# A two-layer decoder step in one Trainium2 kernel: in the second cross attention, VectorE takes the low part of each query projection one tile later

## What is computed

```
q = (queries @ Wq).reshape(b, s, KV_HEADS, GROUP, HEAD_DIM)   # 8, 4, 16
k = (keys @ Wk).reshape(b, s, KV_HEADS, HEAD_DIM)
v = (values @ Wv).reshape(b, s, KV_HEADS, HEAD_DIM)
scores = einsum('bqhgd,bkhd->bhgqk', q, k) * scale
attn = softmax(scores, axis=-1)
out = einsum('bhgqk,bkhd->bqhgd', attn, v).reshape(b, s, 512)
x = x + out @ Wo
```

## Time and profile before

| | |
|---|---|
| median of three runs | 2592.67 us (2592.54 to 2593.83) |
| the profiled execution, its own time | 2595.24 us |
| span of the profile | 2593.5 us |
| mean granted TensorE clock | 0.975 of full speed |
| busy: PE, PEld, DVE, ACT, POOL | 2462.0, 2090.9, 1304.4, 935.9, 732.1 us |
| the second cross attention's four pairs in the trace | about 2330 to 2547 us |

### The profile page before, as it was taken

How to read it: one execution, slowest core, us unless ns; L and a number is a source line. 1 busy time by engine, 2 the same in 40 slices (tenths; PEclk the granted TensorE clock), 3 DMA queues, 4 the chain that set the end, 5 groups by cost and what they waited for, 6 DMA issues and landing times.

```text
span 2593.5 us, 39558 instructions
## 1 busy us (share of the span) xinstructions
PE 2462.0 (95%) x13371; PEld 2090.9 (81%) x13371; DVE 1304.4 (50%) x2997; ACT 935.9 (36%) x2495; POOL 732.1 (28%) x434
## 2 busy tenths in 40 slices
PE   5999899999999999977799999999999999998897
PEld 3788788889888888966688888888888888875665
DVE  6444444444444444564544444444444444567675
ACT  2111344444444444430233333333333333336672
POOL 4245432222322223221211111121111211126660
PEclk9999899999999999988899999999999999997998
DMA  3110221111211121101111111111111111100000
GB/s 111 57 45 28 90 81 49 65 49 56 74 49 65 49 73 57 53 21 43 41 43 42 42 42 42 42 42 42 42 42 42 42 42 42 59 1 1 1 1 33
DMA packets 36976, 119.49 MB, mean 46 GB/s; under 512 B 4920, under 2 KB 7352, under 8 KB 36928
## 3 DMA queue, kind: packets, MB, share of 16 engines
q1 hardware_dynamic: 36928, 118.88, 13.0%
HBM read 116.76 MB, written 2.10 MB: 46 GB/s over the span
## 4 chain that ended last, share of the span: by engine, by line
PE 86%; DVE 7%; issue 3%; POOL 2%; ACT 2%; SPq 0%; DMA 0%; DVEq 0%; POOLq 0%; ACTq 0%
PE pj L521 18%; PE pj L522 18%; PE pj L523 18%; PE ou L521 6%; PE ou L523 6%; PE ou L522 6%; PE sc L655 2%; PE sc L757 2%; PE pv L766 2%; PE pv L671 2%; DVE probs L1257 1%; PE tp L662 1%; PE tp L872 1%; POOL w_lo L393 1%; PE sc L521 1%
## 5 line engine op out<-in xcount | busy, mean ns | idle before, releaser
L385 POOL TENSOR_TENSOR w_lo<-raw,w_hi 128x1024 fp32r<-128x1024 f32 x144 | 344.5, 2392 | 1451.1 <-ACT w_hi L968 1451.1
L521 PE MATMUL pj<-xt_hi,w_hi 128*128 128x512 f32 (+2 forms) x1296 | 519.4, 401 | 7.6 <-POOL w_lo L393 2.0
L522 PE MATMUL pj<-xt_lo,w_hi 128*128 128x512 f32 (+2 forms) x1296 | 502.5, 388 | 0.0
L523 PE MATMUL pj<-xt_hi,w_lo 128*128 128x512 f32 (+2 forms) x1296 | 501.6, 387 | 0.0
L521 PEld LDWEIGHTS pj<-xt_hi,w_hi 128*128 128x128 f32 x1296 | 246.8, 190 | 54.3 <-issue 6.2
L521 PE MATMUL ou<-w_hi,act_hi 128*128 128x512 f32 x684 | 275.4, 403 | 13.1 <-DVE act_lo L1495 4.8
L523 PEld LDWEIGHTS pj<-xt_hi,w_lo 128*128 128x128 f32 x1296 | 245.8, 190 | 49.8
L522 PEld LDWEIGHTS pj<-xt_lo,w_hi 128*128 128x128 f32 x1296 | 246.9, 191 | 41.8
L1216 DVE TENSOR_TENSOR x<-x,ou 128x512 f32<-128x512 f32 (+1 forms) x200 | 136.3, 685 | 285.0 <-PE ou L523 285.0
L523 PE MATMUL ou<-w_hi,act_lo 128*128 128x512 f32 x684 | 268.5, 393 | 0.0
L522 PE MATMUL ou<-w_lo,act_hi 128*128 128x512 f32 x684 | 268.0, 392 | 0.0
(11 more groups left out here) (247 smaller groups left out, 4902.0 us busy)
## 6 DMA issues: line engine op xcount, KB each, us to landing
raw<-in_l1a_w SPq DMA_DIRECT2D x80, 512.0 KB, 4.8
raw<-in_l0x_w SPq DMA_DIRECT2D x64, 512.0 KB, 3.4
side<-in_side SPq DMA_DIRECT2D x32, 512.0 KB, 3.7
raw<-in_ffn_w SPq DMA_DIRECT2D x15, 512.0 KB, 3.2
raw<-in_l1x_w SPq DMA_DIRECT2D x7, 512.0 KB, 3.4
raw<-in_l0f_w SPq DMA_DIRECT2D x6, 512.0 KB, 3.9
raw<-in_taylor_w SPq DMA_DIRECT2D x5, 512.0 KB, 6.6
x<-in_x SPq DMA_DIRECT2D x2, 1024.0 KB, 6.6
```

Of the source, the lines that this page charges most:

```text
L385: pool.tensor_tensor(WL[:, s, :], RAW[:, s, :], f32(WH[:, s, :]), ALU.subtract).then_inc(w_ready[s], 1)
L521: pe.matmul(out, wh, xh, start=first, stop=False)
L522: pe.matmul(out, wh, xl, start=False, stop=False)
L523: return pe.matmul(out, wl, xh, start=False, stop=last)
```

## The change

VectorE's call of `queries` moves by one step in each of its four places in a boundary between pairs: c0 from step 11 to step 12, c1 from 13 to 14, c2 from 15 to step 0 of the next pair, and c3 from step 1' to step 2'. It stands, as before, behind `turned_lo` of its step and ahead of `heads`, `dequantise` and `add`. The index of c2's call is 2 in the next pair in place of 6 in the former: the same projection, bank and columns. No instruction is added or removed; ScalarE, TensorE, GpSimd and SyncE keep their orders. Three boundaries with four calls each make 12 instructions that move.

```diff
@@ -1656,10 +1656,10 @@
                     row_recip(m)
                     if not (first and m < 2):
                         turned_lo(m - 2)
-                    if m == 1 and not first:
-                        queries(3)
-                    if m in (11, 13, 15) and not last:
-                        queries(KC + (m - 11) // 2)
+                    if m in (0, 2) and not first:
+                        queries(2 + m // 2)
+                    if m in (12, 14) and not last:
+                        queries(KC + (m - 12) // 2)
                     if m == 3 and not first:
                         heads(-1)
                     if m == 11:
```

## The result

The changed kernel takes 2581.97 us (median of five runs, 2580.19 to 2584.34) against 2592.67 us (five runs, 2589.14 to 2594.57): 10.7 us less by the medians. The ratio is 0.9955, with a 95% interval of 0.9944 to 0.9967, which is 8.6 to 14.5 us. Forecast were 11.1 us and 2581.6. Its profiled execution took 2582.41 us, with a span of 2580.6, 12.9 us less than before's profiled one.

What follows compares the result with a forecast made beforehand. TensorE bounds the kernel; its boundary waits and lags (10.2 + 1.1 + 0.8) make 12.1 us. Less 3 x 0.34 kept by GpSimd's cycle, the gain is 11.1: 2592.67 - 11.1 = 2581.6 us, range 2577.6 to 2588.

Steps and rivals of the forecast that it cites:

- R: Rival in the single-stall experiments: VectorE's idle time counts, each stall by its share of a boundary's 9.8 us; no chance given.
- (1): VectorE's 12 moved low parts, one step later, wait for nothing: 0 us each, bounds 0 and 0.2.
- (2): First stall, step 12: TensorE's transposes follow their scores after 0.89 us, so the 0.97 us are gone entirely.
- (3): Second stall, 4.33 us under the output projection: its cost shows two steps later, in step 15; 1.9 us gained so far.
- (4): Stalls three and four: GpSimd's 2.33 us cycle leaves 0.34 us a boundary; scores of step 5 start 4.0 us earlier.
- (5): Later readers of the moved low parts on TensorE: cover of 7, 4.5, 4.6 and 3.4 us for c0 to c3.
- (6): Left as they are: waits of 0.63 and 0.37 us inside pairs 1 and 2, and all outside the stretch.
- The rule weighed: VectorE and GpSimd share a port pair: `neg_max` waits for GpSimd's product, 0.99 instead of 0.17 us; without it, 2580.6 us.
- Rival A: Steps 12 to 4': GpSimd's cycle takes over, `neg_max` held in all nine; gain 5.5, 2587.2 us; chance 14%.
- C: TensorE's transposes wait for GpSimd's product or the exponentials instead of `turned_lo`; gain near 0, 2592 us; chance 12%.
- B: Step 15's wait stays, made by `add(0)`; gain 8.5, 2584.2 us; counted within the forecast's case, 69% together.
- D: VectorE steps 12, 14, 0, 2: low part delays `row_max`, `neg_max` meets GpSimd product; 9.1 us slower, 2601.8 us; chance 5%.

Runs made afterwards that it cites:

- ScalarE earlier: Against the kernel before: VectorE's order kept, ScalarE makes each high part one step earlier (10, 12, 14, 0); 2582.89 us, ratio 0.996.
- doubled low part: Against the changed kernel: each of the 12 moved low parts computed twice, the first time into memory that nothing reads; 2581.78 us, ratio 0.9956.
- two steps later: Against the changed kernel: low parts one step later still (steps 13, 15, 1, 3); 2580.38 us, ratio 0.9953.
- no `neg_max`: Against the changed kernel: `neg_max` and its semaphore removed, query projections scaled by -1/4, row minimum as bias of the exponentials; 2581.17 us, ratio 0.9954.
- `add` later: Against the changed kernel: in pairs 1 and 2 the addition of the former pair's last output moves from step 6 to step 10; 2580.43 us, ratio 0.9949.
- both: Against the changed kernel: `neg_max` removed and, in pairs 1 and 2, add(-1) moved from step 6 to step 10; 2582.33 us, ratio 0.9957.

## Why the prediction was right, step by step

- **The bound.** That only TensorE's waits can be won held: 10.97 us were won at the boundaries of the 12.1 counted there, and R, which counts VectorE's 27.0 us, fell in both directions (c1 0.9 a boundary for 4.33 us of stall, c3 1.3 for 1.73). The 12.1 itself was 0.3 too high: the 10.97 won and the 0.80 kept (below) make 11.8, as the lags outside the boundary that was read were smaller than the 0.25 estimated.
- **(1) The stall goes, for 0 us.** The 12 waits have no row after; `turned_lo` and the low part run back to back at 2424.33 and 2424.93, and ScalarE's high part had ended at 2424.56, 0.37 us before the low part starts. That nothing but the high part's coming first matters is shown by the run with ScalarE earlier.
- **(2) and (3).** Step 12: 0.97 forecast, 0.97 measured at the second boundary. Up to step 15: 1.9 us forecast, 1.86 measured (0.97 in step 12, 0.86 in step 15 and 0.03 between).
- **(4) The rest.** 4.0 forecast, 4.01 measured at the second boundary. What was kept back, 0.34 us, was in fact one wait of 0.23 (0.29 by the starts); the lags of 0.11 and 0.15 in steps 3 and 4 did not come. At the first and third boundary the measured 3.47 and 3.49 are what their brackets and lags gave, less the one wait for keys that stayed (0.29 and 0.22 by the starts). So 0.80 us was kept in all, not 1.02. The sum of 11.1 against 10.97 is right by its terms, but that it comes within 0.1 us is luck: 0.3 too much counted and 0.2 too much kept back. That the medians, which scatter by a few us, differ by just 10.7 is luck too.
- **(5) The readers.** Cover of 7, 4.5, 4.6 and 3.4 us was forecast, and the trace of the changed kernel has 7.1, 4.6, 4.6 and 3.5 at the second boundary. Two steps of delay against the kernel before are free, and three cost 5.0 to 5.2 us a boundary beyond the change where the clock stays up. Right.
- **(6).** The 0.63 and 0.37 us inside the pairs stayed to the hundredth.
- **The rule weighed.** `neg_max` is held by GpSimd's products less than I thought: of the nine in steps 12 to 4' of the second boundary five took 0.17 us and four 0.33 to 0.45. The sign that I named, `neg_max` near 1 us more often, went the other way: eight lasted 0.99 to 1.04 us in the stretch of the earlier trace rows, and two in the changed kernel's 123 us. Rival A's cycle ran in four of the nine steps, 0' and 2' to 4', where GpSimd's products stand 2.32 or 2.33 us behind the last (rows of steps 2' to 4' below, timeline of POOL, changed kernel), and TensorE lost 0.29 us to it. By the Trainium skill's rule that I named ("SBUF — State Buffer", Who interferes with whom) the second to issue blocks until the first is done, and the trace agrees: the lengthened `neg_max` of step 3' ends at 2446.31, 0.03 us behind GpSimd's product for the keys (last two rows below, POOL and DVE), and the three others end 0.03 to 0.04 us behind theirs. Taking `neg_max` away gave 1.4 us in the trace.

```profile
2444.24 1.04 POOL L504 TENSOR_TENSOR probs<-probs,row_recip 128x512 f32<-128x512 f32 x1 [0.29 <-DVE row_recip L1628]
...
2446.57 1.04 POOL L504 TENSOR_TENSOR probs<-probs,row_recip 128x512 f32<-128x512 f32 x1 [0.29 <-DVE row_recip L1628]
...
2448.90 1.04 POOL L504 TENSOR_TENSOR probs<-probs,row_recip 128x512 f32<-128x512 f32 x1 [0.29 <-DVE row_recip L1628]
...
2445.24 1.04 POOL L492 TENSOR_TENSOR keys_hi<-ctx_hi,block_mask 128x512 fp32r<-128x512 f32 x1
...
2445.86 0.45 DVE L1623 TENSOR_SCALAR neg_max<-row_max 128x4 f32<-128x4 f32 x1
```

- **The rivals.** All four fell: A and C because one wait a boundary, of 0.15 to 0.23 us, is left in the changed kernel's trace, B by the run of c1 alone and D by the doubled low part.
- **What was missed.** The prediction took the clock of the stretch as safe. With part of the stalls left it is not (below). The kernel before may be exposed to it too and the changed one not, which no term of the sum has; that part is not shown.

## What to carry to other kernels

When an in-order engine waits for a result that another engine makes at the end of the same step, the wait is worth what the late work behind it in the queue delays on the bounding engine, not its own length: read the next instruction of that kind on the bounding engine and compare its start with an undisturbed step. A consumer that is moved behind the instruction which already waits for the producer's predecessor costs nothing, as long as its own reader is further off; count that cover in steps at both ends. Stalls that end on another engine's event swallow whatever was gained ahead of them, so remove a row of them together and do not judge them one by one.

## What the runs showed of the hardware

Short waits of TensorE can cost several times their length through the clock, and not every time. In the kernels with c0, c1 or c2 alone moved, the waits of step 2 stay (about 0.4 and 1.0 us, or about 1.4 alone). Behind them five of the nine boundaries in the profiled executions have a stretch at the lower level: two with c0 moved, one with c1, two with c2. Each cost 2.4 to 4.2 us. A sixth, shorter one (1.6 us) stands behind the wait of 1.49 us in the kernel with the low parts three steps later. With c3 moved, alone or with c2, the wait of 1.0 us is gone, and none of the six boundaries has one. In the six kernels with all four stalls gone and no new wait (ScalarE earlier, two steps later, doubled low part, no `neg_max`, `add` later, both) and in the changed kernel, the stretch from 2380 to 2500 us was granted 1.00 throughout.

The runs of the kernel before went up to 2600.18 us beside its median of 2594.06 in one set of 31, those of the changed kernel, five only, stayed within 2580.19 to 2584.34. That such falls make before's longer times is likely, but its own profiled execution has none in this stretch, so it is not shown; nor is what decides between a fall and none at the same two waits.

The clock varies in pair 0 as well, ahead of the change: the 40 us from 2340 us were granted between 0.62 and 0.86 in the profiled executions, without any order to it. From the first scores of pair 0 to those of step 12 the kernels gained between 0 and 3.3 us on the kernel before's profiled execution. That is a scatter in every comparison of this kernel, larger than most of what the later experiments looked for.
